# The two-of-sixteen expert choice: four working tensors as bf16, experts outside and tiles inside

## The chip, the cores and the metric

One core of a Trainium2 chip runs the whole program. The metric is the device time of one execution in microseconds (us), before and after one change, each as a median of several runs. One execution of the kernel before was also taken by the hardware profiler; its trace is what the numbers here are read from. VectorE is called DVE in the trace, ScalarE ACT, TensorE PE (its weight loads PEld), GpSimd POOL and SyncE SP.

## The reference, cut to what matters

The input is a batch of 16 images of 64 channels and 32 by 32 pixels. A layer norm over the channels, two convolutions with signs for weights and inputs, and a residual come first. Each pixel is then a token of 64 numbers, 16,384 in all. A second layer norm is followed by a feed-forward block with 16 experts, of which each token uses two:

```python
logits = jnp.einsum('bsd,de->bse', x, gate_w) + gate_b
probs = jax.nn.softmax(logits, axis=-1)
top_probs, top_idx = jax.lax.top_k(probs, 2)
top_probs = top_probs / jnp.sum(top_probs, axis=-1, keepdims=True)
dispatch = jnp.sum(jax.nn.one_hot(top_idx, n_experts, dtype=x.dtype) * top_probs[..., None], axis=-2)
...
hidden = jax.nn.silu(h1) * h2
expert_out = jnp.einsum('bseh,eho->bseo', hidden, w3)
return jnp.einsum('bseo,bse->bso', expert_out, dispatch)
```

The change touches the step in which the two largest of a token's 16 logits are found; of equal logits the one with the lower number counts as the larger.

## The kernel before, in words

**Pairs.** The images are worked on in 8 pairs. A pair is 2 times 1024 tokens, which stand as 128 partitions by 16 tiles. The convolution half is a software pipeline: in step `t` of a loop each engine does one part of pair `t`, another of pair `t-1`, and so on to `t-4`. All engines have their own program, written out by hand, and wait on semaphores; nothing reorders it. In one step DVE does, in this order: `weights` and, after `first_choice` of another pair, `slots` (the page row of each token of pair `t-4`), `second_choice` of pair `t-3`, `channels` and `score` (the logits) of pair `t-2`, `places`, the second convolution's result (`conv2`, line 1190) and the residual (line 1197) of pair `t-1`, and the norm of pair `t`.

**The choice.** `first_choice(q)` is a chain of dependent DVE instructions, each over 16 tiles by 16 experts, so 256 elements a partition: the largest logit of each tile (`best`, line 1258), where it stands (`match`, 1236), times a rank that falls with the expert's number (`key`, 1239), the largest key (1242), where that stands (`pick1`, 1244), and the picked logit is pushed to the bottom (1265). `second_choice(q)` repeats this on what is left (1274, 1236, 1239, 1242, 1244) and ends with `chosen = pick1 - pick2` (1290). Three small instructions of another pair's Newton step (lines 1207, 1213, 1218) stand between those of the second choice. The first of them to be awaited elsewhere is 1213, right after the second `match`: PE's product with the gate weights (line 818) waits for it.

**Pages.** After the choice, PE turns and counts the chosen experts, DVE's `slots` gives each token a row of a page (ends with `slot_int`, line 1376), and POOL scatters the tokens into pages in memory, 16 scatters a pair, 128 in all (line 523). The feed-forward half then works through 147 pages of 128 tokens (lines 947, 948: up; 1557: `hide`; 962: down). PE begins on the pages of the first pairs while the last two pairs are still being placed: `second_choice` of pair 6 stands on DVE's program after the `hide` of page 0, `first_choice` of pair 7 after that of page 2, `slots` of pair 6 and then `second_choice` of pair 7 before that of page 6. POOL scatters pairs 6 and 7 behind the others. SP loads page 40 and those after it when all 128 scatters have landed (lines 398 to 400).

Of the kernel before, what the change touches and what calls it, by code (L numbers as in the profile page):

```python
# [5 lines left out]
ALU = mybir.AluOpType  # L6
ACT = mybir.ActivationFunctionType
AX = mybir.AxisListType
F32 = mybir.dt.float32
F32R = mybir.dt.float32r  # L10
BF16 = mybir.dt.bfloat16
# [4 lines left out]
P = 128  # L16
# [3 lines left out]
MASKED = -3.0e38  # L20
# [30 lines left out]
def metaformer_kernel(nc, x, w1, gamma1, beta1, mean1, var1, w2, gamma2, beta2, mean2, var2,  # L51
                      gate_w, gate_b, ffn_w1, ffn_w2, ffn_w3, out):
    B, C, H, W = x.shape
    E, D, HID = ffn_w1.shape
    _, _, KH, KW = w1.shape
    HW = H * W
    PAIRS = B // 2
# [4 lines left out]
    TILES = 2 * CH * TPC  # L62
# [22 lines left out]
    with ExitStack() as ctx:  # L85
        def sb(name, shape, dt):
            return ctx.enter_context(nc.sbuf_tensor(name, shape, dt))
# [4 lines left out]
        def sem(name):  # L92
            return ctx.enter_context(nc.semaphore(name))
# [17 lines left out]
        minus_half = sb("minus_half", [P, TILES], F32)  # L111
        gate_mat = sb("gate_mat", [P, 2, E], F32)
        gate_bias = sb("gate_bias", [P, E], F32)
        first_rank = sb("first_rank", [P, E], F32)
        rank_int = sb("rank_int", [P, E], I32)
        place_int = sb("place_int", [P, 1], I32)
        place_bits = sb("place_bits", [P, 8], I32)
# [43 lines left out]
        blank = blank.rearrange("p (r w) -> p r w", w=ROW)  # L161

        logits = [sb(f"logits{i}", [P, TILES, E], F32) for i in range(2)]
        match = sb("match", [P, TILES, E], F32)
        key = sb("key", [P, TILES, E], F32)
        pick1 = sb("pick1", [P, TILES, E], F32)
        pick2 = sb("pick2", [P, TILES, E], F32)
        best = sb("best", [P, 4, TILES], F32)
        gap = sb("gap", [P, TILES], F32)
        gap_tanh = sb("gap_tanh", [P, TILES], F32)  # L170
        chosen = sb("chosen", [P, TILES, E], BF16)
# [92 lines left out]
        pool_made, dve_made, tables_made = sem("pool_made"), sem("dve_made"), sem("tables_made")  # L264
# [22 lines left out]
        chosen_ready, chosen_turned, chosen_read = sem("chosen_ready"), sem("chosen_turned"), sem("chosen_read")  # L287
# [721 lines left out]
        def _(dve):  # L1009
# [9 lines left out]
            for zeroed in (sign1[:, :, :], sign2[:, :, :], conv_w[:, :, :, :]):  # L1019
                dve.memset(zeroed, 0.0).then_inc(dve_made, 1)  # L1020
            dve.wait_ge(pool_made, PM_GATE)
            dve.tensor_copy(first_rank[:, :], rank_int[:, :]).then_inc(dve_made, 1)

            raw = bn_raw[:, :].rearrange("p (k v) -> p k v", k=2)

# [145 lines left out]
            def then(ins):  # L1171
                nonlocal links
                links += 1
                ins.then_inc(route_link, 1)

            def settled(back=0):
                dve.wait_ge(route_link, links - back)

            def spread(a, n):
                return a.unsqueeze(2).to_broadcast([P, TILES, n])  # L1180
# [48 lines left out]
                                  rstd[:, 1, half].unsqueeze(2).to_broadcast([P, TILES // 2, C]), ALU.mult)\  # L1229
                    .then_inc(channels_ready[0], 1)  # L1230

            def ranks():
                return first_rank[:, :].unsqueeze(1).to_broadcast([P, TILES, E])

            def matches(n, q):
                then(dve.tensor_tensor(match[:, :, :], logits[q % 2][:, :, :], spread(best[:, n, :], E), ALU.is_equal))

            def keys(n):
                then(dve.tensor_tensor(key[:, :, :], match[:, :, :], ranks(), ALU.mult))

            def pick_key(n, pick):
                then(dve.tensor_reduce(best[:, 2 + n, :], key[:, :, :], AX.X, ALU.max))
                settled()
                then(dve.tensor_tensor(pick[:, :, :], key[:, :, :], spread(best[:, 2 + n, :], E), ALU.is_equal))
                settled()

            def score(q):
# [8 lines left out]
            def first_choice(q):  # L1256
                settled()
                then(dve.tensor_reduce(best[:, 0, :], logits[q % 2][:, :, :], AX.X, ALU.max))
                settled()
                matches(0, q)  # L1260
                settled()
                keys(0)
                settled()
                pick_key(0, pick1)
                then(dve.scalar_tensor_tensor(out=logits[q % 2][:, :, :], in0=pick1[:, :, :], scalar=MASKED,
                                              in1=logits[q % 2][:, :, :], op0=ALU.mult, op1=ALU.add))


            def second_choice(r, b):
                q = r  # L1270
                settled()
                if r:
                    dve.wait_ge(chosen_turned, r)
                then(dve.tensor_reduce(best[:, 1, :], logits[q % 2][:, :, :], AX.X, ALU.max))
                if b < PAIRS:
                    newton_slack(1, b)
                settled()
                matches(1, q)
                if b < PAIRS:
                    newton_sum(1, b)  # L1280
                else:
                    settled(1)
                dve.tensor_tensor(gap[:, :], best[:, 0, :], best[:, 1, :], ALU.subtract).then_inc(gap_ready, 1)
                settled()
                keys(1)
                if b < PAIRS:
                    newton_root(1, b)
                settled()
                pick_key(1, pick2)
                dve.tensor_tensor(chosen[:, :, :], pick1[:, :, :], pick2[:, :, :], ALU.subtract).then_inc(chosen_ready, 1)  # L1290

            def places(q):

# [189 lines left out]
            for t in range(PAIRS + 1):  # L1483
                a, s, b, r, z = t, t - 1, t - 2, t - 3, t - 4
                if z >= 0:
                    weights(z)
                if 0 <= r < PAIRS:
                    first_choice(r)
# [104 lines left out]
            for n in range(PAGES + LAG + 2):  # L1593
# [23 lines left out]
                if n in back_step:  # L1617
                    q, c = back_step[n]
# [31 lines left out]
```

## Time and profile before

| what | us |
|---|---|
| time before, median of 3 runs | 532.3 (528.3 to 535.14) |
| the profiled execution, its own time | 528.8 |
| its span, first to last instruction | 526.8 |
| DVE busy, share of the span | 397.1 (75%) |
| PE busy, share of the span | 473.7 (90%) |

The profiled execution lies near the fastest of the three runs, 3.5 us under their median; 2.0 us of it lie outside the span. The busy shares are means over a convolution half, in which several engines take turns, and a feed-forward half from about 191 us on, in which PE has work nearly all the time.

### The profile page before, as it was taken

What the parts mean: (1) busy time and instruction counts of PE and PEld (TensorE: products, weight loads), DVE (VectorE), ACT (ScalarE), POOL (GpSimd) and SP (SyncE); (2) the same over time, 40 slices, a digit from 0 to 9 for tenths busy, and PEclk for the clock granted to TensorE, in tenths of its full rate; (3) what the DMA queues carried; (4) which work ended last, traced back from release to release, by engine and by line L of the source; (5) the groups of instructions that cost most, each with busy time, mean ns of one, the idle gap of its engine ahead of it and who ended that gap; (6) DMA issues with size and microseconds to landing.
All of it is one profiled execution on the core that took longest, in us unless ns stands there. A gap on an engine that the chain in (4) does not pass through costs nothing.

```text
span 526.8 us, 15132 instructions
## 1 busy us (share of the span) xinstructions
PE 473.7 (90%) x4774; PEld 416.0 (79%) x4774; DVE 397.1 (75%) x917; ACT 257.0 (49%) x461; POOL 284.2 (54%) x378
## 2 busy tenths in 40 slices
PE   6889989898996858689999999999999999999983
PEld 6557667665774558679998999999999999999982
DVE  5457787988888779888766777777877778777783
ACT  4467788976884543224343443443434434344320
POOL 4000006877777777677777754445444454445652
PEclk9689899998998879789999999999999999999996
DMA  6981011020200343011213332232333524211034
GB/s 263 330 159 42 0 42 55 32 67 28 69 30 29 85 94 81 26 32 43 57 36 80 79 72 52 47 87 56 88 97 87 137 53 127 58 34 54 25 124 160
DMA packets 62664, 41.03 MB, mean 78 GB/s; under 512 B 50003, under 2 KB 54318, under 8 KB 62080
## 3 DMA queue, kind: packets, MB, share of 16 engines
q1 hardware_dynamic: 52208, 23.84, 19.7%
q0 software_dynamic: 8800, 8.94, 5.3%
q10 hardware_dynamic: 1584, 7.29, 3.4%
q8 instruction: 45, 0.74, 0.6%
q14 instruction: 27, 0.22, 0.1%
HBM read 21.46 MB, written 19.19 MB: 77 GB/s over the span
## 4 chain that ended last, share of the span: by engine, by line
PE 64%; DVE 14%; POOL 8%; issue 8%; ACT 3%; DMA 2%; SPq 1%; POOLq 0%; DVEq 0%; ACTq 0%
PE turn L962 21%; PE up L947 10%; PE up L948 10%; PE up L772 8%; POOL pages L523 5%; PE small L789 4%; POOL results L511 3%; PE small L818 3%; PE small L857 2%; PE up L747 2%; PE turn L801 1%; PE lines L969 1%; ACT rstd_wide L587 1%; DVE up_w L1166 1%; PE turn L862 1%
## 5 line engine op out<-in xcount | busy, mean ns | idle before, releaser
L511 POOL DMA_INDIRECT results<-result,page_in x147 | 146.7, 998 | 117.9 <-ACT xc L702 87.1
L523 POOL DMA_INDIRECT pages<-payload,slot_int x128 | 131.4, 1026 | 107.3 <-DVE slot_int L1376 69.5
L702 ACT ACTIVATE xc<-up,gate_unscale 128x512 f32<-128x512 f32 x147 | 101.2, 688 | 179.5 <-PE up L948 157.5
L947 PE MATMUL up<-xs_hi,up_w 128*128 128x128 f16 x1176 | 150.1, 221 | 7.6 <-DVE sq L1557 3.2
L948 PE MATMUL up<-xs_lo,up_w 128*128 128x128 f16 x1176 | 150.1, 221 | 0.0
L947 PEld LDWEIGHTS up<-xs_hi,up_w 128*128 x1176 | 124.1, 106 | 8.4 <-issue 8.3
L948 PEld LDWEIGHTS up<-xs_lo,up_w 128*128 x1176 | 116.6, 99 | 0.1
L1557 DVE SCALAR_TENSOR_TENSOR hidden<-up,hidden_scale,xc 128x512 f32<-128x512 f32 x74 | 55.5, 749 | 37.3 <-ACT xc L702 34.6
L962 PE MATMUL turn<-down_raw,sq 128*128 x584 | 80.2, 281 | 1.6 <-DVE branch L1568 0.4
L962 PE MATMUL turn<-down_raw,hidden 128*128 x592 | 78.1, 275 | 1.4 <-issue 0.4
L962 PEld LDWEIGHTS turn<-down_raw,sq 128*128 128x128 f32 x584 | 71.6, 193 | 9.2 <-issue 6.9
L962 PEld LDWEIGHTS turn<-down_raw,hidden 128*128 128x128 f32 x592 | 72.2, 193 | 6.3 <-issue 5.4
L1557 DVE SCALAR_TENSOR_TENSOR sq<-up,hidden_scale,xc 128x512 f32<-128x512 f32 x73 | 54.5, 747 | 21.2 <-ACT xc L702 19.5
L772 PE MATMUL up<-sign,conv_w 128*128 128x512 bf16 x192 | 53.2, 435 | 0.0
L772 PEld LDWEIGHTS up<-sign,conv_w 128*128 128x128 bf16 x192 | 21.1, 116 | 25.9 <-issue 11.1
L789 PE MATMUL small<-mean_col,sq 128*128 128x2 f32 x256 | 32.4, 257 | 6.1 <-ACT sq L613 3.5
L789 PEld LDWEIGHTS small<-mean_col,sq 128*128 128x128 f32 x256 | 31.8, 201 | 7.2 <-ACT sq L613 4.1
L1568 DVE TENSOR_TENSOR branch<-turn,page_in 128x512 f32<-128x512 f32 (+1 forms) x38 | 25.9, 683 | 6.2 <-PE turn L962 6.1
L1568 DVE TENSOR_TENSOR rstd_wide<-turn,page_in 128x512 f32<-128x512 f32 x36 | 24.8, 689 | 5.8 <-PE turn L962 5.7
L695 ACT ACTIVATE xs_hi<-small 128x512 f16<-128x512 f32 (+1 forms) x36 | 21.4, 594 | 9.7 <-PE small L857 9.6
L1475 DVE SCALAR_TENSOR_TENSOR xs_lo<-small,xs_hi 128x512 f16<-128x512 f32 (+1 forms) x36 | 24.3, 676 | 0.0
L857 PE MATMUL small<-ident,page_in 128*128 128x128 f32 x143 | 22.7, 283 | 0.8 <-DMA page_in<-pages 0.8
(238 smaller groups left out, 598.0 us busy)
## 6 DMA issues: line engine op xcount, KB each, us to landing
pages<-x ACTq DMA_DIRECT2D x4, 1332.0 KB, 10.8
page_in<-pages SPq DMA_DIRECT2D x147, 36.0 KB
page_in<-pages SPq DMA_DIRECT2D x147, 32.0 KB
x_in<-in_x SPq DMA_DIRECT2D x7, 512.0 KB, 3.5
out<-up_raw SPq DMA_DIRECT2D x5, 512.0 KB, 2.9
results<-result,page_in POOLq DMA_INDIRECT x147
up_raw<-in_L_ffn_w SPq DMA_DIRECT2D x4, 512.0 KB, 17.1
pages<-payload,slot_int POOLq DMA_INDIRECT x128, 2.2
```

Of the source, the lines that this page charges most:

```text
L511: pool.indirect_dma_start(out=results, out_offset=bass.IndirectOffsetOnAxis(ap=page_in[g % LOADS][:, k, D + AT_TOKEN:D + AT_TOKEN + 1].bit ...
L523: pool.indirect_dma_start(out=pages, out_offset=bass.IndirectOffsetOnAxis(ap=slot_int[q % PAYLOADS][:, t:t + 1], axis=0), in_=payload[q % ...
L702: act.activation(act_s[n % 2], up[n % 2][:, 0:CW], ACT.Silu, scale=gate_unscale[:, 0:1])\
L772: last = pe.matmul(cv[c], conv_w[:, which, t, :], image[:, c * ROWS + i:(c + 1) * ROWS + i, j:j + W], start=(t == 0), stop=(t == len(TAPS) ...
L789: last = pe.matmul(var_ps[n][:, 2 * j:2 * j + 2], sq[:, j * P:(j + 1) * P], mean_col[:, :], start=True, stop=True)
L857: last = pe.transpose(rows_bank(g)[:, k * P:(k + 1) * P], page_in[g % LOADS][:, k, 0:2 * D], ident[:, :])
L947: pe.matmul(target, own, xs_hi[g % 2][:, at], start=True, stop=False)
L948: last = pe.matmul(target, own, xs_lo[g % 2][:, at], start=False, stop=True)
L962: last = pe.matmul(target, hidden[n % RING][:, at], whole[:, bass.ds(e, D)], start=True, stop=True)
L1475: dve.scalar_tensor_tensor(out=xs_lo[g % 2][:, 0:width], in0=rows_bank(g)[:, 0:width], scalar=X_SCALE, in1=xs_hi[g % 2][:, 0:width], op0=A ...
L1557: dve.scalar_tensor_tensor(out=hidden[n % RING], in0=up[n % 2][:, CW:HW], scalar=hidden_scale[:, 0:1], in1=act_s[n % 2], op0=ALU.mult, op1 ...
L1568: dve.tensor_tensor(weighed[g % 2][:, k:k + count, :, :], down_pair(m)[:, 0:count, :, :], weights.unsqueeze(3).to_broadcast([P, count, PER ...
```

## The change

`match`, `key`, `pick1` and `pick2` become bf16 and change their layout from 16 tiles by 16 experts (experts next to each other) to 16 experts by 16 tiles (tiles next to each other). `by_tile` gives the old order of such a tensor as a view, in which neighbours lie 16 elements of 2 bytes apart. Through that view `match` is written, `key` is reduced, `pick1` is read when the picked logit is masked, and `pick1` and `pick2` are read when `chosen` is made. The multiplication that makes `key` and the comparison that makes a pick have three operands of bf16 each, all with tiles innermost. For that the ranks, which were one row of 16 numbers, read again for each tile, are now written out in full as `ranks`, once at the start, and the largest key has a bf16 tensor of its own, `best_key`. The logits, their largest (`best`) and `chosen` stay as they were.

No instruction is added, removed or moved: each engine has the same instructions in the same order, and the line numbers of the functions below `best` grow by one or two.

```diff
@@ -111,7 +111,6 @@
         minus_half = sb("minus_half", [P, TILES], F32)
         gate_mat = sb("gate_mat", [P, 2, E], F32)
         gate_bias = sb("gate_bias", [P, E], F32)
-        first_rank = sb("first_rank", [P, E], F32)
         rank_int = sb("rank_int", [P, E], I32)
         place_int = sb("place_int", [P, 1], I32)
         place_bits = sb("place_bits", [P, 8], I32)
@@ -161,11 +160,13 @@
         blank = blank.rearrange("p (r w) -> p r w", w=ROW)
 
         logits = [sb(f"logits{i}", [P, TILES, E], F32) for i in range(2)]
-        match = sb("match", [P, TILES, E], F32)
-        key = sb("key", [P, TILES, E], F32)
-        pick1 = sb("pick1", [P, TILES, E], F32)
-        pick2 = sb("pick2", [P, TILES, E], F32)
-        best = sb("best", [P, 4, TILES], F32)
+        match = sb("match", [P, E, TILES], BF16)
+        key = sb("key", [P, E, TILES], BF16)
+        pick1 = sb("pick1", [P, E, TILES], BF16)
+        pick2 = sb("pick2", [P, E, TILES], BF16)
+        best = sb("best", [P, 2, TILES], F32)
+        best_key = sb("best_key", [P, 2, TILES], BF16)
+        ranks = sb("ranks", [P, E, TILES], BF16)
         gap = sb("gap", [P, TILES], F32)
         gap_tanh = sb("gap_tanh", [P, TILES], F32)
         chosen = sb("chosen", [P, TILES, E], BF16)
@@ -1019,7 +1020,7 @@
             for zeroed in (sign1[:, :, :], sign2[:, :, :], conv_w[:, :, :, :]):
                 dve.memset(zeroed, 0.0).then_inc(dve_made, 1)
             dve.wait_ge(pool_made, PM_GATE)
-            dve.tensor_copy(first_rank[:, :], rank_int[:, :]).then_inc(dve_made, 1)
+            dve.tensor_copy(ranks[:, :, :], rank_int[:, :].unsqueeze(2).to_broadcast([P, E, TILES])).then_inc(dve_made, 1)
 
             raw = bn_raw[:, :].rearrange("p (k v) -> p k v", k=2)
 
@@ -1229,19 +1230,20 @@
                                   rstd[:, 1, half].unsqueeze(2).to_broadcast([P, TILES // 2, C]), ALU.mult)\
                     .then_inc(channels_ready[0], 1)
 
-            def ranks():
-                return first_rank[:, :].unsqueeze(1).to_broadcast([P, TILES, E])
+            def by_tile(a):
+                return a[:, :, :].rearrange("p e t -> p t e")
 
             def matches(n, q):
-                then(dve.tensor_tensor(match[:, :, :], logits[q % 2][:, :, :], spread(best[:, n, :], E), ALU.is_equal))
+                then(dve.tensor_tensor(by_tile(match), logits[q % 2][:, :, :], spread(best[:, n, :], E), ALU.is_equal))
 
             def keys(n):
-                then(dve.tensor_tensor(key[:, :, :], match[:, :, :], ranks(), ALU.mult))
+                then(dve.tensor_tensor(key[:, :, :], match[:, :, :], ranks[:, :, :], ALU.mult))
 
             def pick_key(n, pick):
-                then(dve.tensor_reduce(best[:, 2 + n, :], key[:, :, :], AX.X, ALU.max))
-                settled()
-                then(dve.tensor_tensor(pick[:, :, :], key[:, :, :], spread(best[:, 2 + n, :], E), ALU.is_equal))
+                then(dve.tensor_reduce(best_key[:, n, :], by_tile(key), AX.X, ALU.max))
+                settled()
+                then(dve.tensor_tensor(pick[:, :, :], key[:, :, :],
+                                       best_key[:, n, :].unsqueeze(1).to_broadcast([P, E, TILES]), ALU.is_equal))
                 settled()
 
             def score(q):
@@ -1262,7 +1264,7 @@
                 keys(0)
                 settled()
                 pick_key(0, pick1)
-                then(dve.scalar_tensor_tensor(out=logits[q % 2][:, :, :], in0=pick1[:, :, :], scalar=MASKED,
+                then(dve.scalar_tensor_tensor(out=logits[q % 2][:, :, :], in0=by_tile(pick1), scalar=MASKED,
                                               in1=logits[q % 2][:, :, :], op0=ALU.mult, op1=ALU.add))
 
 
@@ -1287,7 +1289,7 @@
                     newton_root(1, b)
                 settled()
                 pick_key(1, pick2)
-                dve.tensor_tensor(chosen[:, :, :], pick1[:, :, :], pick2[:, :, :], ALU.subtract).then_inc(chosen_ready, 1)
+                dve.tensor_tensor(chosen[:, :, :], by_tile(pick1), by_tile(pick2), ALU.subtract).then_inc(chosen_ready, 1)
 
             def places(q):
 
```

## Rows read from the trace of the kernel before

**Rows 1.** The page: busy time by engine; the chain that ended last, by engine.

```profile
PE 473.7 (90%) x4774; PEld 416.0 (79%) x4774; DVE 397.1 (75%) x917; ACT 257.0 (49%) x461; POOL 284.2 (54%) x378
...
PE 64%; DVE 14%; POOL 8%; issue 8%; ACT 3%; DMA 2%; SPq 1%; POOLq 0%; DVEq 0%; ACTq 0%
```

**Rows 2.** The same chain by time, pair 2's first choice: start us, us, what.

```profile
95.87 0.34 DVE best L1258
...
98.06 0.43 DVE logits L1265
```

**Rows 3.** PE in order of time: start us, us, what, [idle before, and its releaser].

```profile
124.75 1.97 PE L818 MATMUL small<-gate_mat,xc 128*128 128x32 f32 x16 [2.01 <-DVE slack L1213]
...
167.40 0.27 PE L887 MATMUL small<-ident,page_at 128*2 128x128 f32 x1 [4.55 <-DVE slack L1213]
...
191.61 0.29 PE L947 MATMUL up<-xs_hi,up_w 128*128 128x128 f16 x1 [3.12 <-DVE xs_lo L1475]
...
198.49 0.23 PE L947 MATMUL up<-xs_hi,up_w 128*128 128x128 f16 x1 [1.24 <-DVE hidden L1557]
...
214.18 0.39 PE L827 MATMUL lines<-ident_b,chosen 128*128 128x128 bf16 x2 [3.40 <-DVE chosen L1290]
...
280.82 0.66 PE L857 MATMUL small<-ident,page_in 128*128 128x128 f32 x4 [0.79 <-DMA page_in<-pages]
```

**Rows 4.** POOL in order of time: pair 6's first scatter, and the last of all.

```profile
212.29 0.96 POOL L523 DMA_INDIRECT pages<-payload,slot_int  x1 [2.11 <-DVE slot_int L1376]
...
271.59 0.97 POOL L523 DMA_INDIRECT pages<-payload,slot_int  x1 [0.31 <-issue]
```

**Rows 5.** DVE in order of time, columns as in rows 3.

```profile
8.74 1.26 DVE L1054 COPY conv_w<-turn 64x384 bf16<-64x384 bf16 x4 [2.34 <-PE turn L726]
...
84.36 0.42 DVE L1250 TENSOR_TENSOR logits<-small,rstd 128x256 f32<-128x256 f32 x1 [1.42 <-PE small L818]
...
148.91 0.74 DVE L1190 SCALAR_TENSOR_TENSOR bn_sum<-up,bn,x_ln 128x512 f32<-128x512 f32 x1
150.04 0.75 DVE L1190 SCALAR_TENSOR_TENSOR bn_sum<-up,bn,x_ln 128x512 f32<-128x512 f32 x1 [0.39 <-PE up L772]
```

**Rows 6.** Groups of DVE instructions: count | busy us, mean ns of one | idle before.

```profile
L1236 DVE TENSOR_TENSOR match<-logits,best 128x256 f32<-128x256 f32 x16 | 6.8, 426 | 0.3
L1244 DVE TENSOR_TENSOR pick<-key,best 128x256 f32<-128x256 f32 x16 | 6.8, 425 | 0.5
L1239 DVE TENSOR_TENSOR key<-match,first_rank 128x256 f32<-128x256 f32 x16 | 6.7, 421 | 0.3
L1242 DVE TENSOR_REDUCE best<-key 128x16 f32<-128x256 f32 x16 | 6.7, 419 | 0.3
...
L1265 DVE SCALAR_TENSOR_TENSOR logits<-pick,logits 128x256 f32<-128x256 f32 x8 | 3.4, 426 | 0.3
...
L1290 DVE TENSOR_TENSOR chosen<-pick 128x256 bf16<-128x256 f32 x8 | 3.4, 424 | 0.3
...
L1297 DVE TENSOR_REDUCE by_x<-chosen 128x64 f32<-128x256 bf16 x8 | 3.3, 413 | 0.1
...
L1298 DVE TENSOR_REDUCE by_y<-chosen 128x64 f32<-128x256 bf16 x8 | 3.3, 409 | 0.0
...
L1314 DVE TENSOR_SCALAR payload<-token_int 128x16 int32<-128x16 int32 x4 | 0.7, 185 | 0.0
...
L1452 DVE TENSOR_REDUCE pairs_behind<-reached 128x2 f32<-128x16 f32 x2 | 0.4, 178 | 0.0
...
L1578 DVE TENSOR_TENSOR halves<-branch 128x128 f32<-128x128 f32 x1 | 0.3, 291 | 0.0
...
L1395 DVE TENSOR_REDUCE open_count<-begun 128x1 f32<-128x20 f32 x1 | 0.2, 165 | 0.0
```

**Rows 7.** Groups of ACT instructions, columns as in rows 6.

```profile
L544 ACT ACTIVATE conv_sign<-conv_raw 128x384 bf16<-128x384 f32 x2 | 1.7, 884 | 2.5 <-DMA conv_raw<-in_L_conv_w 2.5
...
L695 ACT ACTIVATE xs_hi<-small 128x384 f16<-128x384 f32 x1 | 0.5, 492 | 0.1
```

## The prediction, made before the changed kernel ran

> **What bounds the kernel now.** I read the page first, then the chain of waits, then each engine in order of time. On the page PE is busy for 90% of the span and DVE for 75%; of the chain that ended last DVE holds 14% [rows 1]. Those means hide two halves. From about 281 us on PE has pages without a gap, and no changed instruction runs there: the last choice, that of pair 7, ends by 214 us. What counts is how early two things are done. One is the last scatter, which POOL issues at 271.59 us [rows 4] and for which page 40 and all after it wait. The other is PE's way through pages 0 to 39. They end almost together: when PE comes to turn page 40 at 280.82 us it has waited only 0.79 us for that load [rows 3].
>
> Both go back to DVE. POOL scatters without a break until it waits 2.11 us for the slots of pair 6; the usual gap between two scatters is 0.30 us, as in the last row's 0.31, so 1.81 us of it is a real wait [rows 4]. PE waits for DVE again and again up to 215 us [rows 3]: at the gate product, or what stands ahead of it, for the Newton step inside a second choice (124.75 us for pair 3's, 167.40 us for pair 5's, and alike in pair 2's round), at page 0 for `xs_lo` (191.61), at page 2 for a `hide` behind pair 6's second choice (198.49), and at 214.18 us for pair 7's `chosen`, 3.40 us. So in this stretch the choices are in the path: the whole first choice of pair 2 stands in the chain, instruction by instruction [rows 2].
>
> **The change part by part.** A choice before is a row of instructions of 256 elements at 419 to 426 ns [rows 6].
>
> *Key and pick* become two-input instructions with 16-bit operands, all dense. No row shows such an instruction. Bounds: at one element a cycle they stay at 421 and 425 ns; at two a cycle they stream as long as 128 elements of fp32 do, which take 291 ns [rows 6]. I take 291, since dtype and order of all three operands now allow two at a time: minus 130 and minus 134, together minus 0.264 us a choice.
> The Trainium skill's page "VectorE: DVE Perf Modes" (section "The perf-mode tier table") has `tensor_tensor` at two elements a cycle for bf16 in SBUF and one for fp32; no run here shows it yet.
>
> *The strided reads*: the reduction of `key`, the masking of the logit, and `chosen`. Their elements are now 32 bytes apart. The rows disagree by distance. `by_y` reads bf16 at a step of 8 bytes and takes 409 ns where the dense `by_x` takes 413 [rows 6]: no cost. `conv_sign` on ACT reads fp32 at a step of 24 bytes and takes 884 ns for 384 elements, against 492 ns for 384 dense ones [rows 7]: plus 392 ns, 1.02 ns an element. `pairs_behind` on DVE reads 16 elements at a step of 80 bytes in 178 ns, while 20 dense ones take 165 [rows 6]: at least 13 / 16 = 0.8 ns an element. Steps on both sides of 32 bytes cost about 1 ns, and only the step of 8 bytes costs nothing, so I take 256 times 1.02 ns = 0.261 us each. Bounds: 0, and for `chosen`, which reads two such tensors, twice that, 0.522.
>
> *The strided write* of `match`: the only strided write of single elements is `payload<-token_int`, 16 elements at 288 bytes, 185 ns on the mean [rows 6], too few to tell 0 from 1 ns an element. Bounds 0 and 0.261; I take the middle, 0.13.
>
> So a first choice changes by 0.13 - 0.264 + 0.261 (reduction) + 0.261 (mask) = **+0.39 us**, and a second by 0.13 - 0.264 + 0.261 + 0.261 (`chosen`) = **+0.39 us**. Up to the Newton step that PE waits for, a second choice has only its `match` changed: +0.13.
>
> *The ranks in full*: one conversion of 256 elements instead of 16, once at the start. It costs at most the 0.4 us of any instruction of 256 elements, and DVE then sits idle for 2.34 us before the taps come [rows 5]: nothing. If it were not covered, 0.3 us, once.
>
> Where it lies. Pairs 0 and 1 choose while PE has the longer way: DVE is idle after the second choice, 1.42 us in pair 1's round [rows 5], more in pair 0's; +0.78 us fits in. POOL's first scatter moves by pair 1's first choice, 0.39 us, and has the 1.81 us to spare. In the rounds of pairs 2, 3 and 5 the first choice and the second `match` lie before the gate product that waits (at the waits just named): 3 times (0.39 + 0.13) = 1.56. What is left of those second choices falls into PE's convolution. In pair 4's round both choices push `bn_sum` at 148.91 us, which has no idle time ahead; the next one has 0.39 [rows 5]: 0.78 - 0.39 = 0.39. Then nothing covers DVE: first choice of pair 6 (ahead of `xs_lo`) 0.39, its second (ahead of the `hide` at 198.49) 0.39, first choice of pair 7 (ahead of pair 6's slots) 0.39. Up to pair 6's slots that is 1.56 + 0.39 + 1.17 = **+3.1 us**, and POOL's last scatter moves by as much. PE has pair 7's second choice on top, 3.5 us, but 0.79 us in hand at page 40, so 2.7: POOL's 3.1 decides. After that every page follows as before. The profiled 528.8 us become 531.9; by the median of the runs, 3.5 us higher, 532.3 + 3.1 = **535.4 us**.
>
> **The rivals.**
> *No cost of the stride.* For it speaks `by_y`, the only DVE row with bf16. Then each choice is 0.264 us shorter: the rounds of pairs 2, 3 and 5 and the three choices of pairs 6 and 7 give 6 times 0.264 = 1.6 us, pair 4's round nothing, since PE sets the pace there once DVE is early. POOL's 1.81 us of waiting leaves room for that. 530.7 us. Against it: `conv_sign` and `pairs_behind`.
> *The higher bounds.* Write 0.261 and `chosen` 0.522 make a first choice +0.52, a second +0.78, the `match` +0.26: 3 times 0.78, 1.30 - 0.39, and 0.52 + 0.78 + 0.52 give 5.1 us, 537.4.
> *Key and pick don't double.* The change then does only harm: first and second choice +0.65; 3 times 0.78, 1.30 - 0.39, 3 times 0.65: 5.2 us, 537.5. For it: no row shows a doubled two-input instruction.
> *The 32-byte step costs much more than 1 ns an element.* With x for every strided operation the path gets 3(4x - 0.264) + (6x - 0.528 - 0.39) + 3(3x - 0.264) = 27x - 2.5 us. From x = 0.49 us on (1.9 ns an element, a `match` of 0.91 us) that is 10.6 us, 2% slower, 543 us. Its place is the reads and the write through `by_tile`; for it speaks that a cost by distance exists, against it that the rows at 24 and at 80 bytes show about half of that.
> The Trainium skill's "Vector Engine (DVE) Microarchitecture Reference" (section 5.2, "Measured stream behaviour on trn2") is a rule against this change: a stream runs at full rate only over adjacent 4-byte words in pairs, and a hop at each element raises a column from 1.054 ns to about 1.7, a step of 24 words to 2.5. An estimate from these figures is 0.17 to 0.37 us an operation, which in the formula gives +2.1 to +7.5 us, 534.4 to 539.8. The ACT row lies within it.
>
> **How the numbers follow.** Forecast and its near neighbours, 1 to 5 us slower: 0.55. No cost of the stride: 0.20, 530.7. Higher bounds or no doubling: 0.18, about 537.5. The large step: 0.07, from 541 up to beyond 543. The three runs before spread from 528.3 to 535.14, -4.0 and +2.8 about their median, so a median of few runs moves by 2 us or so. The range goes from 530.7 less 1.7 to 537.5 plus 4, 529 to 541.5, and leaves out most of the large step and the outer part of the spread. 2%, 10.6 us, is about what a measurement of this kernel can tell from no change. Only the large step passes it upward, 0.06 with the spread; a gain of 10.6 us is out of reach, as all the choices' keys and picks together lose 16 times 0.264 = 4.2 us: 0.01. Within 2%: 0.93.
>
> **What the changed profile would show.** Key and pick near 291 ns, reductions, masking and `chosen` near 680, `match` near 555; at 420 for these the first rival holds, at 900 the last. POOL's wait before pair 6's first scatter grows from 2.11 us to about 4.8 (3.1 less the 0.39 of its own start), and the last scatter goes to 274.7 us. If DVE's durations are as said and the last scatter stays, the sum over the path was wrong. It would also be wrong if PE, idle for longer before 215 us, is granted a lower clock for longer behind it; I have put nothing in for that.

## The result, and the profile after

The changed kernel takes 546.3 us, the median of five runs (540.4 to 547.8), against 532.3 before: a ratio of 1.028, 95% interval 1.023 to 1.034. That is slower by more than 2%. The prediction was 535.4 us with a range up to 541.5: it had the sign, and a size about 11 us too small. The time lies where its rival of the large step put it. Executions of one kernel differ by some per cent (the kernel before ran from 526 to 542 us in the sets of the experiments below), and all ratios are taken over the undisturbed ones. The profiled execution of the changed kernel is the fastest of its five, 540.4 us with a span of 538.7; against the profiled 528.8 us before, the trace shows 11.6 us of the 14.

The groups of DVE instructions of the changed kernel come first (count | busy us, mean ns of one | idle before), to be held against rows 6:

```profile
L1237 DVE TENSOR_TENSOR match<-logits,best 128x256 bf16<-128x256 f32 x16 | 19.9, 1245 | 0.3
...
L1243 DVE TENSOR_REDUCE best_key<-key 128x16 bf16<-128x256 bf16 x16 | 9.8, 615 | 0.3
...
L1292 DVE TENSOR_TENSOR chosen<-pick 128x256 bf16<-128x256 bf16 x8 | 5.0, 624 | 0.3
L1267 DVE SCALAR_TENSOR_TENSOR logits<-pick,logits 128x256 f32<-128x256 bf16 x8 | 4.9, 618 | 0.3
...
L1240 DVE TENSOR_TENSOR key<-match,ranks 128x256 bf16<-128x256 bf16 x16 | 4.7, 292 | 0.4
L1245 DVE TENSOR_TENSOR pick<-key,best_key 128x256 bf16<-128x256 bf16 x16 | 4.7, 292 | 0.6
```

`key` and `pick` are at the 291 ns that were forecast. The strided reads pay 192 to 200 ns each, under the 261 taken for them. The strided write of `match` pays 1245 - 426 = 819 ns, where 130 was taken and 261 was the bound. A first choice is longer by 0.819 - 0.129 - 0.133 + 0.196 + 0.192 = 0.945 us, a second (with `chosen`, +0.200, for the mask) by 0.953, and the `match` ahead of the Newton step alone by 0.82.

PE in order of time, the changed kernel: the gate products (the product with the gate weights, line 818 before and 819 now) in the rounds of pairs 1 to 5, the one after them, and PE's longest waits for DVE up to 227 us (idle before, and its releaser, in brackets). A round is named, as in the prediction, for the pair whose second choice falls into it, and "pair 2's gate product" is the one that waits in that round; its own tokens are those of the pair behind it.

```profile
81.29 1.87 PE L819 MATMUL small<-gate_mat,xc 128*128 128x32 f32 x16
...
103.99 2.47 PE L819 MATMUL small<-gate_mat,xc 128*128 128x32 f32 x16 [2.05 <-DVE slack L1214]
...
128.45 2.99 PE L819 MATMUL small<-gate_mat,xc 128*128 128x32 f32 x16 [3.63 <-DVE slack L1214]
...
152.18 1.97 PE L819 MATMUL small<-gate_mat,xc 128*128 128x32 f32 x16 [1.25 <-DVE slack L1214]
...
175.86 0.37 PE L888 MATMUL small<-ident,page_at 128*2 128x128 f32 x1 [6.22 <-DVE slack L1214]
176.03 3.46 PE L819 MATMUL small<-gate_mat,xc 128*128 128x32 f32 x16
...
195.57 1.97 PE L819 MATMUL small<-gate_mat,xc 128*128 128x32 f32 x16 [2.71 <-DVE slack L1214]
...
201.58 0.28 PE L948 MATMUL up<-xs_hi,up_w 128*128 128x128 f16 x1 [4.03 <-DVE xs_lo L1477]
...
227.16 0.39 PE L828 MATMUL lines<-ident_b,chosen 128*128 128x128 bf16 x2 [4.25 <-DVE chosen L1292]
```

The same view of the kernel before, for the gate products that rows 3 leave out:

```profile
82.46 1.87 PE L818 MATMUL small<-gate_mat,xc 128*128 128x32 f32 x16
...
103.55 1.97 PE L818 MATMUL small<-gate_mat,xc 128*128 128x32 f32 x16 [0.44 <-DVE slack L1213]
...
145.49 1.87 PE L818 MATMUL small<-gate_mat,xc 128*128 128x32 f32 x16
...
167.51 2.92 PE L818 MATMUL small<-gate_mat,xc 128*128 128x32 f32 x16
...
186.52 1.97 PE L818 MATMUL small<-gate_mat,xc 128*128 128x32 f32 x16 [2.56 <-DVE slack L1213]
```

The waits named in rows 3 are longer: 2.01 became 3.63, 4.55 became 6.22, 3.12 became 4.03, 3.40 became 4.25. Only the one at page 2 is 1.24 us as before (209.40 us); the wait for pair 6's `chosen` just ahead of it went from 0.28 to 1.74 us instead. Then POOL, pair 6's first scatter and the last of all, against rows 4:

```profile
224.35 1.17 POOL L524 DMA_INDIRECT pages<-payload,slot_int  x1 [6.74 <-DVE slot_int L1378]
...
284.23 0.97 POOL L524 DMA_INDIRECT pages<-payload,slot_int  x1 [0.30 <-issue]
```

The last scatter comes 12.64 us later, and page 40, turned at 280.82 us before, follows at 292.74, 11.92 later. Behind it the page stream is as long as before: span less page 40 is 526.8 - 280.8 = 246.0 before and 538.7 - 292.7 = 246.0 after. The whole loss was made by then.

Not all of it is time of DVE. The windows from a gate product to the variance product that follows it (line 789 before, 790 now; this stretch is called the gate stretch below), first the kernel before for pairs 2, 3, 4 and 5 (stretch, its length, busy us and count of PE, PEld, DVE, ACT and POOL, granted clock, DMA share, GB/s), then the same of the changed kernel:

```profile
103.50:108.30 4.80, 4.75 (x32) 3.28 (x33) 4.48 (x13) 3.83 (x13) 3.77 (x4) 1.00 0.08 25
124.70:131.20 6.50, 6.45 (x33) 3.71 (x33) 4.62 (x13) 2.36 (x11) 4.98 (x6) 0.74 0.07 23
145.40:150.20 4.80, 4.80 (x35) 3.30 (x33) 4.31 (x12) 4.27 (x15) 3.85 (x4) 1.00 0.10 31
167.40:180.60 13.20, 11.55 (x57) 7.53 (x58) 9.15 (x24) 6.60 (x17) 10.04 (x10) 0.74 0.32 72
```

```profile
103.99:110.20 6.21, 6.21 (x31) 3.85 (x31) 4.67 (x11) 2.29 (x10) 4.68 (x6) 0.73 0.09 31
128.45:136.30 7.85, 7.85 (x31) 4.67 (x31) 4.67 (x11) 1.75 (x8) 5.09 (x6) 0.57 0.09 28
152.18:156.74 4.56, 4.56 (x30) 3.08 (x31) 4.46 (x11) 2.96 (x11) 3.34 (x5) 1.00 0.07 24
175.86:189.40 13.54, 11.95 (x54) 8.01 (x55) 9.17 (x24) 6.44 (x17) 8.92 (x10) 0.71 0.28 66
```

PE is busy nearly throughout in the first two of each, with the same work. Pair 2's stretch goes from 4.56 us (gate product to variance product, in the list by time) to 6.21 as the granted clock falls from 1.00 (2.4 GHz) to a mean of 0.73, part of it at 1.2 GHz (0.50 from 105.5 to 107.0 us): ahead of it PE was idle for 2.05 us instead of 0.44. Pair 3's goes from 6.22 to 7.85, with a clock of 0.57 instead of 0.74 behind 3.63 us of idleness instead of 2.01. Pair 4's does not fall behind 1.25 us, and pair 5's grows by 0.40.

With both terms the trace closes, each row within 0.2 us; the clock's term is read from this same trace. The column "worked out" uses the prediction's own path (first choice and second `match` ahead of a gate product; the 0.39 us of cover in pair 4's round) with the measured durations, and puts the longer stretch of the round before to it:

| from | to | before | after | longer by | worked out |
|---|---|---|---|---|---|
| pair 1's gate product | pair 2's | 21.09 | 22.70 | 1.61 | 0.945 + 0.82 = 1.77 |
| pair 2's | pair 3's | 21.20 | 24.46 | 3.26 | 1.77 + 1.65 clock = 3.42 |
| pair 3's | pair 4's | 20.74 | 23.73 | 2.99 | 1.90 - 0.39 + 1.63 clock = 3.14 |
| pair 4's | pair 5's | 22.02 | 23.85 | 1.83 | 1.77 |
| pair 5's | the next | 19.01 | 19.54 | 0.53 | 0.40 clock |
| the next | pair 6's first scatter | 25.77 | 28.78 | 3.01 | 3 x 0.95 = 2.85 |
| sum | | | | 13.23 | 13.35 |

Pair 1's gate product itself comes 1.17 us earlier in the changed kernel's profile, so 13.23 - 1.17 = 12.06, the distance between pair 6's first scatters of the two. Why it comes earlier is not shown; over all kept traces it starts anywhere from 80.83 to 87.19 us.

### The profile page after: what moved, and what is told of

Same layout as the page of the kernel before. It is cut to its first block, busy times and chain, and to the rows that moved or that the text cites. A ratio compares the mean times of both kernels' runs of the same rounds, so it can differ in the third digit from the quotient of the medians.

```text
span 538.7 us, 15132 instructions
## 1 busy us (share of the span) xinstructions
PE 475.4 (88%) x4774; PEld 416.0 (77%) x4774; DVE 411.7 (76%) x917; ACT 256.9 (48%) x461; POOL 282.6 (52%) x378
## 4 chain that ended last, share of the span: by engine, by line
PE 61%; DVE 15%; POOL 8%; issue 8%; DMA 4%; ACT 3%; SPq 2%; POOLq 0%; DVEq 0%; ACTq 0%
PE turn L963 21%; PE up L948 10%; PE up L949 10%; PE up L773 7%; POOL pages L524 5%; PE small L790 3%; PE small L819 3%; POOL results L512 3%; DMA x_in<-in_x 3%; PE small L858 2%; DVE match L1237 2%; PE up L748 1%; PE lines L970 1%; DVE up_w L1167 1%; ACT rstd_wide L588 1%
## 5 line engine op out<-in xcount | busy, mean ns | idle before, releaser
L773 PE MATMUL up<-sign,conv_w 128*128 128x512 bf16 x192 | 54.9, 446 | 0.0
L790 PE MATMUL small<-mean_col,sq 128*128 128x2 f32 x256 | 31.0, 252 | 6.8 <-ACT sq L614 3.5
L790 PEld LDWEIGHTS small<-mean_col,sq 128*128 128x128 f32 x256 | 30.3, 194 | 7.8 <-ACT sq L614 4.1
L819 PE MATMUL small<-gate_mat,xc 128*128 128x32 f32 x128 | 18.5, 303 | 9.6 <-DVE slack L1214 9.6
L819 PEld LDWEIGHTS small<-gate_mat,xc 128*128 128x128 f32 x128 | 18.2, 224 | 11.3 <-DVE slack L1214 11.1
```

The costliest lines, as they stand in the source:

```text
L773: last = pe.matmul(cv[c], conv_w[:, which, t, :], image[:, c * ROWS + i:(c + 1) * ROWS + i, j:j + W], start=(t == 0), stop=(t == len(TAPS) ...
L790: last = pe.matmul(var_ps[n][:, 2 * j:2 * j + 2], sq[:, j * P:(j + 1) * P], mean_col[:, :], start=True, stop=True)
L819: last = pe.matmul(gate_ps[:, j * 2 * E:(j + 1) * 2 * E], xc2[:, j * P:(j + 1) * P], gate_mat[:, :, :].rearrange("p a e -> p (a e)"), star ...
```

## The experiments

The theory: the write of `match` at a step makes most of DVE's loss, and TensorE's lower clock behind the longer waits adds to it. The rivals: the strided reads or the layout as a whole do it; or DVE's time doesn't matter and something else of the change does. All ratios are to the kernel before, run in the same set on the same chip.

**Only the write of `match` undone.** `key` reads it through the view instead.

```diff
-        match = sb("match", [P, E, TILES], BF16)
+        match = sb("match", [P, TILES, E], BF16)
-                then(dve.tensor_tensor(by_tile(match), logits[q % 2][:, :, :], spread(best[:, n, :], E), ALU.is_equal))
+                then(dve.tensor_tensor(match[:, :, :], logits[q % 2][:, :, :], spread(best[:, n, :], E), ALU.is_equal))
-                then(dve.tensor_tensor(key[:, :, :], match[:, :, :], ranks[:, :, :], ALU.mult))
+                then(dve.tensor_tensor(key[:, :, :], match[:, :, :].rearrange("p t e -> p e t"), ranks[:, :, :], ALU.mult))
```

> The changed kernel, but match is written densely (tiles outside) and key reads it through the strided view. Theory: writing single 2-byte elements 32 bytes apart is what costs, 1245 ns where the strided reads cost 615. Then match falls to about 425 ns and key rises from 292 to about 615, each choice is 0.5 us shorter and the time comes to 4 to 9 us under the changed kernel's, ratio to before 1.008 to 1.018. Rival: the step costs as much on whichever side it lies, then key takes 1.2 us and the ratio stays at 1.02 or more.

Measured: 537.0 us, ratio 1.0147 (1.0094 to 1.0199), span 531.8, so about half of the loss is gone. Its groups of DVE instructions:

```profile
L1240 DVE TENSOR_TENSOR key<-match,ranks 128x256 bf16<-128x256 bf16 x16 | 9.8, 613 | 0.3
L1237 DVE TENSOR_TENSOR match<-logits,best 128x256 bf16<-128x256 f32 x16 | 6.8, 425 | 0.3
```

Where `match` was written at the step for 819 ns more, `key` now reads it at the same step for 613 - 292 = 321 ns more, of which about 130 is the lost doubling. The price goes by the side of the access: the same step on the same 2-byte tensor costs 819 ns written and about 190 ns read.

**Only the element size of that write changed.**

```diff
-        match = sb("match", [P, E, TILES], BF16)
+        match = sb("match", [P, E, TILES], F32)
```

> The kernel after with match kept in fp32, still with experts outside, so it is still written at a step of 16 elements, now 64 bytes; key then reads one fp32 and one bf16 operand. Theory (the price of writing match is a price of writing 2-byte elements one by one at a step; 4-byte elements are written whole): match falls from 1245 ns to about 425 to 650 ns, key rises from 292 to about 425 ns, the other strided reads stay at 615 to 624 ns; net some 0.5 to 0.7 us a choice less than in the kernel after, about 537 to 541 us. Rival (any element written away from its neighbour pays a hop, whatever its size): match stays at about 1240 ns, key rises to 425, about 547 us.

Measured: 536.2 us, ratio 1.0102 (1.0019 to 1.0185), span 530.7. Groups of DVE instructions:

```profile
L1237 DVE TENSOR_TENSOR match<-logits,best 128x256 f32<-128x256 f32 x16 | 9.5, 593 | 0.3
L1240 DVE TENSOR_TENSOR key<-match,ranks 128x256 bf16<-128x256 f32 x16 | 6.9, 428 | 0.3
```

Written as 4-byte elements at twice the distance, the same instruction takes 593 ns instead of 1245. The theory holds for the durations, and the rival's 1240 does not come; the time is just under the 537 to 541 us that were expected. The distance in bytes has changed here too; the probes below compare the two types at equal distances.

**The price by itself.** Behind the work of the kernel before stand VectorE operations on a scratch tile; `at(type, first, step)` is a view of 256 elements. The edit is written in short, one line for a series of probes:

```diff
+  tensor_tensor(at(BF16, 4096, step), at(F32, 0, 1), at(F32, 256, 1), ALU.is_equal)   # step 1, 2, 4, 8, 16, 32; 17, 18
+  tensor_tensor(at(F32, 4096, step), at(F32, 0, 1), at(F32, 256, 1), ALU.is_equal)    # step 1, 2, 4, 8, 16; 9, 15
+  tensor_tensor(at(F32, 4096, 1), at(BF16 or F32, 0, step), at(F32, 4352, 1), ALU.is_equal)
+  tensor_copy(at(BF16, 4096, 16), at(F32, 0, 1))
+  tensor_copy(at(F32, 4096, 8), at(F32, 0, 1))
```

> The kernel before, with VectorE operations of 128 x 256 elements added behind its work that only write or only read a scratch tile at steps of 1 to 32 elements, in bf16 and fp32. Theory (a 2-byte element that is written away from its neighbour costs extra, from some step on): dense writes about 425 ns, bf16 writes rise with the step to about 1245 ns at a step of 32 bytes, fp32 writes at the same byte step well under that; reads about 290 to 490 ns at any step. Rival 1 (the price goes by the byte step alone): bf16 and fp32 writes at equal byte steps cost the same. Rival 2 (the price comes of the step 16 being a power of two): steps of 17 or 18 elements cost much less than 16.

The groups, the costliest first: bf16 writes at steps of 8, 17, 16 and 4 elements (L1650, 1659, 1651, 1649), a copy with a bf16 write at 16 (L1673), an fp32 write at 4 (L1655), a bf16 read at 8 (L1665), a bf16 read at 4 (L1664), an fp32 write at 2 (L1654) and a copy with an fp32 write at 8 (L1674):

```profile
L1650 DVE TENSOR_TENSOR x<-x 128x256 bf16<-128x256 f32 x1 | 1.3, 1290 | 0.0
...
L1659 DVE TENSOR_TENSOR x<-x 128x256 bf16<-128x256 f32 x1 | 1.2, 1239 | 0.0
L1651 DVE TENSOR_TENSOR x<-x 128x256 bf16<-128x256 f32 x1 | 1.2, 1229 | 0.0
L1649 DVE TENSOR_TENSOR x<-x 128x256 bf16<-128x256 f32 x1 | 0.7, 724 | 0.0
L1673 DVE CAST x<-x 128x256 bf16<-128x256 f32 x1 | 0.7, 700 | 0.0
...
L1655 DVE TENSOR_TENSOR x<-x 128x256 f32<-128x256 f32 x1 | 0.6, 610 | 0.0
...
L1665 DVE TENSOR_TENSOR x<-x 128x256 f32<-128x256 bf16 x1 | 0.6, 605 | 0.0
...
L1664 DVE TENSOR_TENSOR x<-x 128x256 f32<-128x256 bf16 x1 | 0.4, 426 | 0.0
...
L1654 DVE TENSOR_TENSOR x<-x 128x256 f32<-128x256 f32 x1 | 0.4, 425 | 0.0
...
L1674 DVE COPY x<-x 128x256 f32<-128x256 f32 x1 | 0.4, 396 | 0.0
```

At 8 bytes a bf16 write takes 724 ns and an fp32 write 425; at 16 bytes 1290 and 610. So the price does not go by the byte step alone (rival 1), and steps of 17 and 18 elements (1239 and 1251 ns) cost what 16 does (rival 2). The theory's part on writes holds, except that the full price is there from 16 bytes on. Its part on reads missed: from 16 bytes on a read costs 160 to 190 ns more, about what a write of 4 bytes costs and what the changed kernel's reads pay. From 16 bytes on all these prices stay within about 6% of each other (bf16 writes 1229 to 1290 ns). They are prices of a comparison of two tensors: a copy with one source, writing at a step of 32 bytes as well, takes 700 ns into bf16 and 396 into fp32. No dense copy stands beside these two, so what the step adds there is not shown.

**DVE's time alone, without the change.** In the kernel before each `match` is made three times.

```diff
             def matches(n, q):
+                for again in range(2):
+                    then(dve.tensor_tensor(match[:, :, :], logits[q % 2][:, :, :], spread(best[:, n, :], E), ALU.is_equal))
+                    settled()
```

> The kernel before, with each match made three times over (the same values, each awaited), so that a choice is 2 x 0.455 = 0.91 us longer and nothing else differs. Theory: the changed kernel is slow because its choices are 0.95 us longer on VectorE, and TensorE, which waits for them, is granted a lower clock behind the longer waits. Then this is slower than before by 10 to 14 us, ratio 1.019 to 1.027, and the stretch from the gate product to the next variance in pair 2's round, 4.7 us before and 6.4 us in the changed kernel, takes 6.4 us here too. Rival: the lost time has to do with the layout or the type in some other way (other engines, scatter, pages); then at most 5 us, ratio under 1.01.

Measured: 546.0 us, ratio 1.0251 (1.0113 to 1.039), against 1.0284 for the change. PE at the gate products of pairs 2 and 3, and POOL at pair 6's first scatter:

```profile
106.56 2.56 PE L818 MATMUL small<-gate_mat,xc 128*128 128x32 f32 x16 [2.20 <-DVE slack L1213]
...
133.55 2.27 PE L818 MATMUL small<-gate_mat,xc 128*128 128x32 f32 x16 [3.18 <-DVE slack L1213]
```

```profile
229.00 0.96 POOL L523 DMA_INDIRECT pages<-payload,slot_int  x1 [7.95 <-DVE slot_int L1379]
```

The windows of the two gate stretches, as above:

```profile
106.56:114.24 7.68, 7.68 (x31) 4.34 (x31) 4.59 (x12) 2.14 (x9) 5.05 (x6) 0.58 0.09 30
133.55:139.76 6.21, 6.21 (x30) 3.70 (x31) 4.49 (x12) 1.75 (x8) 4.79 (x5) 0.73 0.09 30
```

The same waits grow, and the two stretches behind them are 7.68 us (6.4 was expected) and 6.21 us, at granted clocks of 0.58 and 0.73. From pair 1's gate product (83.61 us) to pair 6's first scatter it takes 145.39 us, against 143.06 in the changed kernel and 129.83 before. So 0.91 us of DVE a choice, with no bf16 and no stride, gives a loss of the same size.

**TensorE given work in its waits, changed kernel.** Idle transposes into a free bank of the accumulator stand ahead of the gate product; what they make is not read.

```diff
+                if t in FILL:                                  # {5: 15, 6: 26, 7: 8, 8: 46}
+                    pe.wait_ge(conv1_read, CH * (s + 1))
+                    for n in range(FILL[t]):
+                        pe.transpose(cv[0][:, 0:P], ident[:, :], ident[:, :])
```

> The changed kernel, with idle transposes on TensorE (15, 26, 8 and 46 of them in the rounds of pairs 2 to 5, into a bank that is free there) while it waits for VectorE. Theory: behind a wait of 2 us or more TensorE is granted half its clock, and this is the part of the loss that VectorE's durations leave over, 1.6 us in each of the rounds of pairs 2 and 3. Then gate product and convolution run at the full clock, the stretch behind the gate takes 4.8 us in place of 6.4 in pair 2's round and of 8.1 in pair 3's, and the time is 3 to 7 us under the changed kernel's, ratio to before 1.012 to 1.022. Rival: the clock falls anyway, or that stretch is long for what it waits for; then no change, 1.028.

Measured: 540.2 us, ratio 1.0133 (0.9991 to 1.0275). The gate stretches of pairs 2, 3 and 5 are 4.47, 4.56 and 9.81 us instead of 6.21, 7.85 and 13.55, at a granted clock of 1.00. Windows of pairs 3 and 5, then one ahead of pair 2's gate product, then POOL at pair 6's first scatter:

```profile
133.20:137.80 4.60, 4.60 (x31) 3.12 (x31) 4.49 (x11) 1.75 (x8) 3.38 (x5) 1.00 0.10 28
177.50:187.40 9.90, 8.31 (x60) 5.99 (x59) 9.04 (x25) 6.66 (x17) 7.45 (x9) 1.00 0.30 66
```

```profile
100.00:105.00 5.00, 5.00 (x16) 2.58 (x17) 4.83 (x23) 2.14 (x5) 3.33 (x4) 0.50 0.09 30
```

```profile
223.48 1.18 POOL L525 DMA_INDIRECT pages<-payload,slot_int  x1 [5.73 <-DVE slot_int L1383]
```

With work in the waits these stretches run at the full clock, so it is shown that the fall comes of PE's idleness there. How much of the time it carries is less sure: the interval is wide and overlaps that of the change, and the profiled execution itself, 541.8 us, is no shorter than the changed kernel's 540.4. It started its pairs later (pair 1's gate product at 85.07 us instead of 81.29), and the clock was lost elsewhere: the last window, in an earlier convolution without a fill, stands at 0.50 (1.2 GHz). From pair 1's gate product to pair 6's first scatter it takes 138.41 us against 143.06, so 4.65 us less, where the clock's terms in the table were 3.7.

**The types without the layout.** bf16 tensors in the old order, so that none of them is read or written at a step; the edit is cut to its main lines.

```diff
-        match = sb("match", [P, E, TILES], BF16)      # key, pick1, pick2, ranks alike
+        match = sb("match", [P, TILES, E], BF16)
-                return a[:, :, :].rearrange("p e t -> p t e")
+                return a[:, :, :]
-                                       best_key[:, n, :].unsqueeze(1).to_broadcast([P, E, TILES]), ALU.is_equal))
+                                       spread(best_key[:, n, :], E), ALU.is_equal))
...
```

> The changed kernel's types with the layout of before: match, key, picks, ranks in bf16, tiles outside and experts inside, so that nothing is strided. Theory: key takes 292 ns, chosen 292, match, mask and reduction 410 to 426 as before; pick is 425 or 292, depending on whether an operand that repeats one element 16 times lets two go at a time. Choices are 0.13 to 0.4 us shorter than before and the time is 0.5 to 2.5 us less, ratio 0.995 to 0.999. Rival: bf16 in itself costs something (a conversion on the way in or out); then match or mask are longer than 426 ns and the ratio is above 1.

Measured: 532.9 us, ratio 1.0026 (0.9972 to 1.0081): no difference that can be told from none, so the 0.5 to 2.5 us of the theory are neither shown nor refuted. Groups of DVE instructions:

```profile
L1245 DVE TENSOR_TENSOR pick<-key,best_key 128x256 bf16<-128x256 bf16 x16 | 6.8, 426 | 0.5
...
L1240 DVE TENSOR_TENSOR key<-match,ranks 128x256 bf16<-128x256 bf16 x16 | 4.6, 286 | 0.3
...
L1292 DVE TENSOR_TENSOR chosen<-pick 128x256 bf16<-128x256 bf16 x8 | 2.4, 294 | 0.3
```

`key` and `chosen` fall to 286 and 294 ns without any new layout; only the pick, in which one element of `best_key` is read 16 times in a row, stays at 426. `match` and the mask stay at 427 and 425 ns, so bf16 in itself costs nothing here (the rival). With the strides gone and the types kept, the loss is gone: it hangs on the strided accesses that the new layout needs.

**Towards a version that beats both.** That kernel with fills ahead of the variance product and of the gate product, and the kernel before with the same fills. Shown is the fill ahead of the variance product; the one ahead of the gate product is that of the run above, with the counts given here:

```diff
+                    if t in FILL:                              # {3: 0, 4: 0, 5: 4, 6: 14, 7: 0, 8: 40}
+                        pe.wait_ge(conv2_read, CH * (s - 1) + 1)
+                        for n in range(11):
+                            pe.transpose(cv[0][:, 0:P], ident[:, :], ident[:, :])
                     variance(1, b)
```

> bf16 match, key and pick with tiles outside as in the kernel before (no strided access), and TensorE given idle transposes ahead of the variance product of each round from pair 0's on and ahead of the wait for VectorE's slack, so that it is at work in the waits of 1.2 to 2.0 us. Theory (the granted clock falls after those waits, and the fall costs 1.6 to 3 us in a round): no round's convolution or gate stretch runs at the lower clock, stretches from gate product to variance of about 4.5 us in all of pairs 2 to 4 and about 9.8 in pair 5's; 521 to 526 us, ratio 0.980 to 0.99. Rival (the clock falls for another reason, or the idle transposes take as much as they give): 530 to 535 us, ratio 0.995 to 1.005.

> The kernel before with the same idle transposes and nothing else. Theory (what is gained in the run beside it is the clock, not bf16): ratio 0.983 to 0.99, within 1.5 us of the kernel with bf16 and the same transposes, whose shorter key, less 0.13 us a choice, is at most 2 us in all. Rival (bf16 is what gains): ratio 0.995 to 1.005.

Measured: 530.7 us, ratio 0.996 (0.9885 to 1.0036), and 528.9 us, ratio 0.9972 (0.9915 to 1.0029). Neither can be told from no change, so the times that the two expectations gave, 521 to 526 us and a ratio of 0.983 to 0.99, did not come; their clock was right, since in the second kernel the stretches of pairs 2 to 5 are 4.56, 4.47, 4.46 and 9.81 us. The chain that ended last on that kernel's page, by engine, and POOL in order of time at pair 6's first scatter, at its first write of a page's result, and at the last scatter, show where the gain went:

```profile
PE 59%; POOL 20%; issue 11%; DVE 4%; ACT 3%; DMA 2%; SPq 1%; POOLq 0%; DVEq 0%; ACTq 0%
```

```profile
209.42 0.96 POOL L524 DMA_INDIRECT pages<-payload,slot_int  x1 [0.78 <-DVE slot_int L1385]
...
231.77 1.00 POOL L512 DMA_INDIRECT results<-result,page_in  x1 [1.19 <-issue]
...
270.73 0.96 POOL L524 DMA_INDIRECT pages<-payload,slot_int  x1 [0.30 <-issue]
```

The slots of pair 6 come 2.87 us earlier than before, and POOL is then almost without a wait there (0.78 us, with 0.30 the usual gap). Yet its last scatter is issued only 0.86 us earlier. The other 2 us go behind pair 6's first scatter: 0.89 us more than the usual gap ahead of the first result, and four of the result writes that POOL does between its scatters take 1.3 to 1.5 us, where one did before; why they do is not shown. POOL holds 20% of the chain where it held 8% [rows 1], DVE 4% instead of 14%. So once the 1.81 us of waiting that the prediction counted are nearly used up, POOL is the next bound. No version here beats the kernel before by more than the spread of the runs.

## Why the prediction was wrong, point by point

- *What bounds the kernel*: right. The loss is made ahead of page 40, at the waits that were named, and the pages behind are as long as before.
- *Key and pick*: right, 292 ns each instead of 421 and 425. The Trainium skill's "VectorE: DVE Perf Modes" (section "The perf-mode tier table") has `tensor_tensor` at twice the rate for bf16, and the trace agrees: 292 ns is what half the elements took in fp32, 291 [rows 6].
- *The strided reads*: the mechanism was right, the size a third too high: 0.261 us where 0.19 to 0.20 was measured. `chosen`, which reads two such tensors, pays no more than one, so its bound of 0.522 was not needed.
- *The strided write*: this is the step that failed. "Bounds 0 and 0.261; I take the middle, 0.13" became 0.82. The upper bound was the price of a read of fp32 on another engine, the lower came from 16 elements of 4 bytes; no row showed a write of 2-byte elements at a step, and for these the probes, comparisons of two fp32 tensors as `match` is, show 3.1 to 3.4 ns an element from 16 bytes on, against 0.72 for 4-byte elements at 16 bytes.
- *The sum over the path*: the count of places was right. With the measured durations it gives 1.77 + 1.77 + 1.51 + 1.77 + 2.85 = 9.7 us, where 3.1 was said. `match` stands in that sum 11 times, and 11 x 0.69 = 7.6 us of error; the reads take 1.0 us back.
- *TensorE's clock*: the second failed step. The prediction put "nothing in" for a lower granted clock behind longer idleness, and named it only as what could go wrong. It cost 1.65 + 1.63 + 0.40 = 3.7 us in the profiled execution, and the run with work in the waits took the stretches back to full clock. The other four of the five runs took 5.1 to 7.4 us more than the profiled one, at a mean granted clock of 0.916 to 0.924 against 0.940; no trace of them was kept, so where they lost it is not shown.
- *The rival whose time came* is "The 32-byte step costs much more", with a chance of 0.07. Its place was the reads and the write alike; the runs show the write alone, and its sign, reductions, masking and `chosen` at 900 ns, did not come (615 to 624). Its formula used one x for both, so that the reads' rows at 24 and 80 bytes seemed to speak against it, and they say nothing of a 2-byte write. It had no term for the clock either, so that its 543 us lies so near is in part luck. The estimate of 0.17 to 0.37 us an operation that stands beside it fits the reads (0.19 to 0.20) and the write of 4 bytes (593 - 426 ns = 0.17); the write of 2 bytes cost more than twice its upper end.
- *The ranks in full*: the conversion at the start takes 230 ns instead of 111, and the first `key` starts no later for it (56.2 us, before 56.6): nothing, as said.

## What to carry to other kernels

A 16-bit layout that doubles some instructions must be priced over all instructions that touch the tensor: here two faster ones gave 0.26 us a choice, two strided reads took 0.39 back, and the one strided write of 2-byte elements took 0.82. A strided access has a reading and a writing side with different prices, and a row of the one does not bound the other; where no row shows it, the range should stay open upward. Where DVE's delay makes TensorE wait in a stage with little slack, look at the granted clock behind the wait and put a price on its fall as well; and before a gain is hoped for, look for the queue that is next, here POOL with its 128 scatters and the result writes between them.

## What the runs showed of the hardware

- A VectorE comparison of two tensors of 256 elements a partition, about 425 ns dense, takes 605 ns with one of them read as bf16, and 610 with fp32 written, at a step of 16 bytes; at 8 bytes both are free (426 and 425). The Trainium skill's "SBUF — State Buffer" (its note on lines of 16 bytes, section "Door 1: The DMA port swizzle") wants two accesses to a line for full rate, and these rows agree with it. A bf16 write does not: at 8 bytes, two to a line, it takes 724 ns, and from 16 bytes on 1229 to 1290.
- Two strided inputs of one instruction cost what one does: 624 ns for `chosen`, 618 for the mask.
- TensorE's granted clock fell behind waits of 0.85 us (with the write of `match` undone, pair 2's stretch 6.21 us at 0.73) and 2.05 us, and did not fall behind 1.25 us in pair 4's round. Behind 2.71 us, at 195.57 us in the changed kernel, the gate product ran at 0.98, so the theory "behind a wait of 2 us or more" does not hold as it stands. Behind one and the same wait of 1.40 us for ScalarE, ahead of 12 convolution products between pair 1's and pair 2's gate product, these took 2.80 us in the traces before and after, and 5.11 and 5.15 us in those with fills in the changed kernel and with the types alone. The length of the wait alone does not decide it here, and what does is left open.
